# An attention and expert kernel: the first two units' start written out engine by engine, and the first unit's operands moved from SBUF straight to their partitions

## What is computed

```python
# x, ctx: (8, 256, 512); 16 heads of 16 channels
q = Wq @ layernorm(x) + bq;  k = Wk @ ctx + bk;  v = Wv @ ctx + bv
dot = q_head.T @ k_head / 4                      # 512 x 512 per head, masked
x = x + v_head @ (softmax(dot) * mask)
# then, for each of the 2048 rows (8 * 256) of x, with 8 experts:
h = layernorm(x); p = softmax(h @ gate.T); the two best experts, weights normalised
x = x + sum of weight * (silu(h @ w1g) * (h @ w1u)) @ w2
```

## Time and profile before

| | |
|---|---|
| median of 3 runs | 956.54 us (954.77 to 958.49) |
| the profiled execution, own time | 951.4 us |
| its span, first to last instruction | 949.6 us |
| PE busy (matmul) | 810.5 us, 85% |
| DVE busy | 538.6 us, 57% |
| POOL busy | 377.2 us, 40% |
| ACT busy | 316.7 us, 33% |
| mean granted TensorE clock | 0.949 |

### The profile page before, as it was taken

The page is one execution under the profiler, slowest core; times in us unless marked ns, Lnnn a source line. Parts: engine busy times, 40 slices in busy tenths (PEclk is TensorE's granted clock), DMA queues, the critical chain, the costliest instruction groups (busy, mean ns, idle before and its releaser), DMA issues. The chain is left out here.

```text
span 949.6 us, 12844 instructions
## 1 busy us (share of the span) xinstructions
PE 810.5 (85%) x3737; PEld 366.5 (39%) x3738; DVE 538.6 (57%) x1038; ACT 316.7 (33%) x615; POOL 377.2 (40%) x396
## 2 busy tenths in 40 slices
PE   2178999999998999999999983189999999999994
PEld 1022233333332333333333321155555555555552
DVE  2177888888887888887878722412323232322322
ACT  0003656555656555555556672000000000000000
POOL 5634445555755665566554324301111111111111
PEclk9677999999999999999999996589999999999998
DMA  4553467665866676657455322413635365363332
GB/s 120 169 177 113 145 206 222 187 221 177 268 195 193 210 224 197 201 181 210 134 177 156 125 92 90 143 46 67 147 58 155 57 156 146 66 146 62 59 66 34
DMA packets 84287, 137.69 MB, mean 145 GB/s; under 512 B 14600, under 2 KB 40520, under 8 KB 84240
## 3 DMA queue, kind: packets, MB, share of 16 engines
q1 hardware_dynamic: 68512, 107.97, 37.4%
q0 software_dynamic: 7744, 17.86, 9.6%
q10 hardware_dynamic: 7984, 11.28, 4.2%
HBM read 77.34 MB, written 59.36 MB: 144 GB/s over the span
## 5 line engine op out<-in xcount | busy, mean ns | idle before, releaser
L731 DVE TENSOR_REDUCE mx<-tile 128x2 f32<-128x1024 f32 x256 | 308.7, 1217 | 64.8 <-PE tile L985 61.3
L629 ACT ACTIVATE pr<-sc 128x512 f32<-128x512 f32 x512 | 268.8, 601 | 191.5 <-PE sc L972 189.0
L985 PE MATMUL tile<-qk 97*128 97x512 bf16 x512 | 157.2, 390 | 47.6 <-DVE mx L731 22.4
L1283 POOL DMA_INDIRECT out_dram<-y,ids x36 | 56.1, 1559 | 282.5 <-DVE ids L1208 278.4
L972 PE MATMUL sc<-qk 100*128 100x512 bf16 x512 | 154.6, 382 | 7.7 <-DMA qk<-mxt 5.1
L1001 PE MATMUL pvb<-pr,vp 128*32 128x512 f32 x1024 | 137.2, 608 | 0.0
L1263 ACT ACTIVATE sg<-gp 128x352 f32<-128x352 f32 x36 | 16.7, 465 | 291.3 <-PE up L1312 291.3
L1333 PE MATMUL dp<-wring,at 128*128 (+1 forms) x216 | 102.2, 609 | 13.4 <-DVE at L1218 13.4
L985 PEld LDWEIGHTS tile<-qk 97*128 97x128 bf16 x512 | 36.4, 98 | 185.7 <-DVE mx L731 83.0
L1312 PE MATMUL gp<-wring,xtile 128*128 x288 | 93.7, 469 | 2.1 <-DVE meta L1199 2.1
L554 POOL TENSOR_SCALAR parts<-qkf 128x512 bf16<-128x512 f32 x32 | 48.4, 1513 | 113.3 <-DVE qkf L812 112.4
(11 more groups left out here) (118 smaller groups left out, 723.9 us busy)
## 6 DMA issues: line engine op xcount, KB each, us to landing
qk<-stack_d SPq DMA_DIRECT2D x32, 768.0 KB
stack_d<-parts SPq DMA_DIRECT2D x32, 384.0 KB, 2.6
wring<-w_dram SPq DMA_DIRECT2D x32, 352.0 KB, 6.3
xl<-routed_d ACTq DMA_DIRECT2D x38, 257.0 KB, 2.7
stack_d<-parts SPq DMA_DIRECT2D x32, 256.0 KB, 2.9
pv_d<-ov SPq DMA_DIRECT2D x32, 256.0 KB, 4.1
xin<-x_dram SPq DMA_DIRECT2D x16, 256.0 KB, 5.7
cin<-ctxt_dram SPq DMA_DIRECT2D x8, 512.0 KB, 6.2
```

The costliest lines, as they stand in the source:

```text
L629: nc.scalar.activation(pr[s % 2][:, j, :], sc[(32 * u + 4 * s + j) % NSC][:, :], ACT.Exp, scale=SCALE).then_inc(exped.sem, 1)
L731: dve.tensor_reduce(mx[:, half(w), 2 * j:2 * j + 2], t[:, :, :], X, ALU.max, negate=True).then_inc(drained.sem, 1)
L985: last = nc.tensor.matmul(t[:, i, :], qs[half(w)][0:RAW_ROWS, h, c * P:c * P + P], ks[half(w)][0:RAW_ROWS, h, :], start=True, stop=True)
L1283: pool.indirect_dma_start(out, bass.IndirectOffsetOnAxis(ap=ids[:, k, :], axis=0), y[:, k, :], None, compute_op=ALU.add).then_inc(y_added, 16)
```

## The change

`tile_events` gives the tiles of units -2 and -1 in a new order: q and k of unit 1 (called "the second unit") come ahead of every raw score, the values of unit 0 after all its raw scores and the transposed maxima. Each engine's instructions up to unit -1 are written out, in an order of its own. The first unit's parts no longer pass through `stack_d`: SP (q) and ACT (k) start twelve transfers, one for each pair and side, from `parts` into 16 partitions of `qk[0]`, each as soon as its part exists. The first unit's k is split by DVE (`key_parts`), no longer by POOL. The constants that the start needs come first and have semaphores of their own. The five stores of `pad` are moved behind unit 1. SP's `keep_split(-1, 0)` is moved behind the transfer of the maxima. The diff, without its unchanged lines and the new semaphores' names:

```diff
@@ -102,6 +102,11 @@
+    if n == -2:
+        return ["q", "k"] + [("max", m) for m in range(LEAD)]
+    if n == -1:
+        return ([("max", m) for m in range(LEAD, NPAIR)]
+                + ["maxT", "v", ("max", 0), ("max", 1), "q", ("max", 2), ("max", 3), "k"])
@@ -278,8 +288,12 @@
-        split_kept = [Count(sem(f"split_kept{side}"), of(3 - side, "k"), 3 * 16) for side in range(2)]
-        stacked = [Count(sem(f"stacked{g}"), of(2 - g, "g"), 32) for g in range(2)]
+        split_kept = [Count(sem(f"split_kept{side}"), lambda n, w=3 - side: ["k"] if 0 < n + w < UNITS else [], 3 * 16)
+                      for side in range(2)]
+        stacked = [Count(sem(f"stacked{g}"), lambda n, w=2 - g: ["g"] if 0 < n + w < UNITS else [], 32)
+                   for g in range(2)]
+        first_moved = [sem(f"first_moved{side}") for side in range(2)]
+        first_mask = sem("first_mask")
@@ -302,13 +316,13 @@
+        early = ((io[:, :], iotas, io_in),
+                 (wq_s[:, :, :], wq.rearrange("(c p) o -> p c o", p=P), wq_in),
+                 (bqk[:, 0, :], bq, wq_in),
+                 (wk_s[:, :, :], wk.rearrange("(c p) o -> p c o", p=P), wk_in),
+                 (bqk[:, 1, :], bk, wk_in),
+                 (mall[:, :], mask, mask_in))
@@ -316,7 +330,16 @@
-        MADE = 8
+        MADE = 6
+        def first_stack(eng, u, side):
+            for part in range(3):
+                eng.wait_ge(split[side].sem, split[side].at(u, (0, 2, 3)[part]))
+                for i, pair in enumerate(PAIRS):
+                    if pair[side] == part:
+                        eng.dma_start(qk[0][i * D:i * D + D, side, :, :].rearrange("d h t -> d (h t)"),
+                                      parts[:, side, part, :]).then_inc(first_moved[side], 16)
@@ -415,7 +438,7 @@
-                if has(u + 1):
+                if has(u) and has(u + 1):
@@ -442,7 +465,7 @@
-                if has(u + 3):
+                if u >= 0 and has(u + 3):
@@ -454,22 +477,35 @@
-            for u in range(FIRST, -2):
-                unit(u)
-            sp.wait_ge(const_made, MADE)
-            sp.wait_ge(ones_made, 4)
+                if u == -1:
+                    keep_split(u, 0)
+            def pads():
+                for i in range(4):
+                    sp.dma_start(routed_d[E * CAP + i * P:E * CAP + (i + 1) * P, :], pad[:, :]
+                                 ).then_inc(padded, 16)
+                sp.dma_start(out[TOKENS:TOKENS + P, :], pad[:, 0:T]).then_inc(padded, 16)
+            load_x(-5)
+            load_x(-4)
+            load_ctx(-3)
+            sp.wait_ge(mask_made, 2)
+            load_x(-3)
+            load_x(-2)
-            for i in range(4):
-                sp.dma_start(routed_d[E * CAP + i * P:E * CAP + (i + 1) * P, :], pad[:, :]
-                             ).then_inc(padded, 16)
-            sp.dma_start(out[TOKENS:TOKENS + P, :], pad[:, 0:T]).then_inc(padded, 16)
-            for u in range(-2, LAST + 1):
+            sp.wait_ge(ones_made, 1)
+            for g in range(2):
+                sp.dma_start(qk[0][BIAS_ROW:BIAS_ROW + 1, :, 4 * g:4 * g + 4, :], mrow_d[0:1]).then_inc(first_mask, 16)
+            first_stack(sp, -3, 0)
+            keep_split(-2, 0)
+            for u in range(-1, LAST + 1):
+                if u == 1:
+                    sp.wait_ge(const_made, MADE)
+                    pads()
@@ -482,15 +518,15 @@
-            for h in range(2):
+            def ones_of(h):
-            pool.wait_ge(const_loaded, CONST)
+                pool.wait_ge(const_loaded, CONST)
@@ -549,6 +585,8 @@
+                if w == 1:
+                    pool.wait_ge(first_moved[side], 6 * 16)
@@ -576,7 +614,17 @@
-            for u in range(FIRST, LAST + 1):
+            ones_of(0)
+            pool.wait_ge(io_in, 16)
+            batch_rstd(-5)
+            batch_rstd(-4)
+            pool.wait_ge(normed.sem, normed.at(-4, "n"))
+            ones_of(1)
+            part(-3, 0)
+            batch_rstd(-3)
+            batch_rstd(-2)
+            part(-2, 0)
+            for u in range(-1, LAST + 1):
@@ -637,8 +685,12 @@
+            for dst, src, loaded in early:
+                act.dma_start(dst, src).then_inc(loaded, 16)
+            act.wait_ge(ones_made, 1)
+            first_stack(act, -2, 1)
@@ -924,20 +976,69 @@
-            unit(FIRST)
+            def key_parts(u):
+                w = u + 2
+                src = qkf[:, half(w), 1, :]
+                dve.wait_ge(drained.sem, drained.at(u - 1, "k"))
+                dve.tensor_reduce(parts[:, 1, 0, :], src.rearrange("p (t o) -> p t o", o=1), X, ALU.max
+                                  ).then_inc(split[1].sem, 1)
+                dve.wait_ge(split[1].sem, split[1].at(u, 0))
+                dve.tensor_tensor(rest[:, 1, :], src, parts[:, 1, 0, :], ALU.subtract).then_inc(split[1].sem, 1)
+                dve.wait_ge(split[1].sem, split[1].at(u, 1))
+                dve.tensor_reduce(parts[:, 1, 1, :], rest[:, 1, :].rearrange("p (t o) -> p t o", o=1), X, ALU.max
+                                  ).then_inc(split[1].sem, 1)
+                dve.wait_ge(split[1].sem, split[1].at(u, 2))
+                dve.tensor_tensor(parts[:, 1, 2, :], rest[:, 1, :], parts[:, 1, 1, :], ALU.subtract
+                                  ).then_inc(split[1].sem, 1)
-            dve.wait_ge(const_loaded, CONST)
+            for u in (-5, -4):
+                batch_stats(u, 0)
+                batch_stats(u, 1)
+            normalize(-5)
+            normalize(-4)
+            dve.wait_ge(mask_in, 16)
+            dve.tensor_copy(mrow[:, 0, :], mall[:, :]).then_inc(mask_made, 1)
+            dve.tensor_scalar(mrow[:, 1, :], mall[:, :], 1.0, NEG / SCALE, ALU.subtract, ALU.mult
+                              ).then_inc(mask_made, 1)
+            dve.wait_ge(io_in, 16)
+            dve.wait_ge(wq_in, 32)
+            projection_out(-3, 0)
+            dve.wait_ge(wk_in, 32)
+            projection_out(-3, 1)
+            key_parts(-2)
+            dve.wait_ge(const_loaded, CONST)
-            dve.tensor_copy(mrow[:, 0, :], mall[:, :]).then_inc(const_made, 1)
-            dve.tensor_scalar(mrow[:, 1, :], mall[:, :], 1.0, NEG / SCALE, ALU.subtract, ALU.mult
-                              ).then_inc(const_made, 1)
-            for u in range(FIRST + 1, LAST + 1):
+            projection_out(-2, 0)
+            projection_out(-2, 1)
+            for u in (-3, -2):
+                batch_stats(u, 0)
+                batch_stats(u, 1)
+            normalize(-3)
+            for j in range(LEAD):
+                maximum(-2, j)
+            normalize(-2)
+            for j in range(LEAD, NPAIR):
+                maximum(-1, j)
+            split_maxima(-1)
+            values_out(-1)
+            maximum(-1, 0)
+            maximum(-1, 1)
+            projection_out(-1, 0)
+            maximum(-1, 2)
+            batch_stats(-1, 0)
+            maximum(-1, 3)
+            batch_stats(-1, 1)
+            normalize(-1)
+            projection_out(-1, 1)
+            for u in range(LAST + 1):
@@ -946,9 +1047,6 @@
-            pe.wait_ge(const_made, MADE)
-            pe.wait_ge(ones_made, 4)
@@ -977,7 +1075,11 @@
-                if m % 8 == 0:
+                if m == 0 and w == 0:
+                    pe.wait_ge(first_mask, 32)
+                    pe.wait_ge(first_moved[0], 6 * 16)
+                    pe.wait_ge(first_moved[1], 6 * 16)
+                if m % 8 == 0 and w:
@@ -1103,7 +1205,27 @@
-            for u in range(FIRST, LAST + 1):
+            pe.wait_ge(wq_in, 32)
+            project(-3, 0)
+            pe.wait_ge(wk_in, 32)
+            project(-3, 1)
+            project(-2, 0)
+            project(-2, 1)
+            for m in range(LEAD):
+                raw_scores(-2, m)
+            for m in range(LEAD, NPAIR):
+                raw_scores(-1, m)
+            pe.wait_ge(const_made, MADE)
+            pe.wait_ge(ones_made, 4)
+            transpose_maxima(-1)
+            values(-1)
+            raw_scores(-1, 0)
+            raw_scores(-1, 1)
+            project(-1, 0)
+            raw_scores(-1, 2)
+            raw_scores(-1, 3)
+            project(-1, 1)
+            for u in range(LAST + 1):
```

More of the change, by code:

```diff
@@ L253, in attention @@
         pvb = st.enter_context(nc.psum_tensor("pvb", [P, T], F32))
+        io_in = sem("io_in")
+        mask_in = sem("mask_in")
+        wq_in = sem("wq_in")
+        wk_in = sem("wk_in")
         const_loaded = sem("const_loaded")
         const_made = sem("const_made")
+        mask_made = sem("mask_made")
         mrow_kept = sem("mrow_kept")
@@ L304, in attention @@
         block = st.enter_context(nc.Block())
-        const = ((idf[:, :], ident),
[L306 to L311, removed]
+        early = ((io[:, :], iotas, io_in),
[4 more added lines that the diff above has]
+                 (mall[:, :], mask, mask_in))
+        const = ((idf[:, :], ident),
                  (wv_s[:, :, :], wv.rearrange("(c p) o -> p c o", p=P)),
```

## The result

The changed kernel takes 947.94 us in the median of six runs (946.11 to 950.63), the kernel before 954.16 (952.79 to 958.49): ratio 0.9927, 95% interval 0.9902 to 0.9953. It is faster by 6.2 us where 25.8 were forecast, and 947.94 lies outside the range of 925 to 941.

A forecast was written before the change was run, and what follows sets the result against it. PE bounds units and experts, so the change is worth what it moves the first score: 25.4 + 7.9 - 5.0 - 2.5 = 25.8 us earlier, 956.5 to 930.7, call it 931; range 925 to 941.

The forecast's parts named there:

- Step 2: First raw score to transposed maxima: 20.6 us after the change against 28.5 before, a gain of 7.9.
- Step 3: Transposed maxima to first score: 12.0 us for 7.0, because values and third unit's q come here; a loss of 5.0.
- Step 4: Second unit's stack, needed for its first raw pair at 45.2, would land at 44.8: hidden by 0.4 us.
- Step 1: Start to first raw score: 22.1 against 47.47, a gain of 25.4 us, with 2.8 for the last transfer's landing.
- Rival B: Transfers landing on sixteen partitions are a narrow door, delaying the first unit's operands: 941 us, chance 0.08.
- Step 5: Unit 0: third unit's q split late, stack(1, 1) behind it, so PE stands before raw pair 8; 2.5 us taken.
- Step 6: Pad stores behind unit 1, ahead of stack(3, 1), which has 7 us spare: cost 0, at most 2 us.
- A: Rival: the second unit's chain decides, its stack 4 us late and unit 0's 4 more: 939 us, chance 0.17.
- D: Rival, slower: unit 0's debt is not paid off and PE stands before raw pair 8 in every unit: 968, chance 0.05.
- C: Rival, no gain: the twelve transfers are served one by one, start unchanged: 956 us, chance 0.04.

The follow-up runs named there:

- the run with ACT's order: The changed kernel, but ACT starts the first unit's six k transfers in pair order 5, 0, 3, 4, 1, 2, not 0, 3, 5, 1, 4, 2: 944.93 us.
- the run without it: The changed kernel, but SP issues stack(1, 1) ahead of keep_split(-1, 0), no longer behind it: 936.98 us, ratio 0.9805.
- The runs with the pads late: Five pad stores issued one to a unit in units 9 to 13: alone on the changed kernel 945.51 us; with stack(1, 1) ahead of keep_split(-1, 0) 936.35.
- the run through DRAM: The changed kernel, but the first unit's parts go through DRAM again, after all parts are made, all on SP: 947.02 us, ratio 0.9885.

## Why the prediction was wrong

**What held.** The mechanism and most terms. PE's start: 8.37 for 7.5 (it waited for a 1 KB bias, not for the weights). POOL's and DVE's parts: 18.8 and 19.3 for 17.9 and 18.7; a reduction over one element takes 0.69, a subtraction 0.69 alone and 1.10 and 1.37 beside POOL, so the overlap cost 0.4 and 0.7 for the 0.4 taken. (A second overlap stood in the kernel before, which the forecast didn't count: at 22.31 a normalisation took 0.54 beside POOL, whose split took 1.74 for 1.50.) The second subtraction ended at 19.31, 0.55 after POOL's own subtraction had ended at 18.76; in three other traces it is 16.25 after 15.71, with 1.29 to 1.66 for the one that waited. That agrees with the lock rule of the Trainium skill (SBUF — State Buffer, Who interferes with whom). The first ended at 17.18, while POOL's split ran from 16.03 to 17.53, which the rule doesn't give. Step 2, first raw to transposed maxima: 20.8 for 20.6. Step 3: 11.7 for 12.0. Step 4: the second unit's stack was issued at 46.65 and PE's first pair with it, at 56.66, did not wait.

**Step 1, the landing.** The term "issue 0.6, landing 2.8" was mis-sized. The transfers took 3.6 to 12.4 us to land, and the first raw score came at 32.3 for 22.1, that is 10.2 of the lost gain: 9.1 between the last issue and the raw score (11.9 for 2.8), the rest in parts and issue that were 1.1 later. The 2.8 came from transfers whose side in SBUF was all 128 partitions; these land on sixteen neighbours. Rival B (0.08) named this. It had two cases at a quarter of 251 GB/s for each quarter of the partitions: the quarters at the same time, 25 and 934, or all twelve transfers in turn, 41.5 and 950, and it took 941, which is a first raw score near 32.4. The measured 32.31 is that value, by luck of the middle: the transfers do share one rate, whichever quarter they go to, but it is 110 GB/s and not 63. The argument that nothing before lands on so few partitions was not quite so: the maxima and the mask rows do, in transfers of 8 KB that show no rate. Spreading the rows gives 8.2 back; the rate is then 229 to 265 GB/s and the time 940.67.

The Trainium skill (SBUF — State Buffer, Door 1: The DMA port swizzle) has 109 GB/s for partitions 0 to 15, and 104 measured; the 104 to 122 of the changed kernel's two traces are near it, at times above it. By its mapping sixteen partitions that are six apart reach 13 or 14 of the 16 ports, an estimated 354 GB/s or more; the 222 to 265 measured agree in kind and not in size. I had used the rule for each transfer's last 1.2 us and not for the queue of twelve. The Trainium skill (SBUF — State Buffer, Can I just issue two DMAs to hit both halves?) also says that two transfers to different halves serialize; the run with ACT's order agrees, 113 GB/s where the changed kernel has 109 to 122. The 150 to 155 GB/s measured with 32 neighbours lie below the 189 that the Trainium skill (SBUF — State Buffer, Door 1: The DMA port swizzle) gives for 32 in transfers of 1 MiB; why is open. What makes neighbours slow is thus shown by position, and the ports as its cause rest on that section of the Trainium skill alone.

**Step 5, the debt in unit 0.** Sized 2.5, measured 8.6 (lead 18.2 to 9.5). The sum for SP was right in kind: `stack(1, 1)` issued 8.2 after the first score (7.7 forecast), landed 14.6 after it (13.4). The need was wrong. I read pair 8 off the pair at 94.42. Counted in the kernel before from 83.83, pair 4, that one is pair 10; pair 8 starts at 91.58, 8.6 after the first score, not 11.4 (pairs 4 to 9):

```profile
83.83 1.06 PE L985 MATMUL tile<-qk 97*128 97x512 bf16 x2
...
85.87 0.60 PE L985 MATMUL tile<-qk 97*128 97x512 bf16 x2
...
86.85 0.60 PE L985 MATMUL tile<-qk 97*128 97x512 bf16 x2
...
88.92 0.60 PE L985 MATMUL tile<-qk 97*128 97x512 bf16 x2
...
91.58 0.59 PE L985 MATMUL tile<-qk 97*128 97x512 bf16 x2
...
93.54 0.60 PE L985 MATMUL tile<-qk 97*128 97x512 bf16 x2
```

With it the same sum gives a stop of 4.8 (13.4 - 8.6), and landing 1.2 later makes it the 6.1, near enough. The other 2.5 I put down to the clock, which stood at half after the stop and at full in the run without it. The forecast had no term for that.

**Step 6, the pads.** Cost 0, at most 2: 1 to 4 in the traces. The same misread row: the 7 us to spare were 4, against 2.5 of issue and 4 to 5 of data. The runs with the pads late moved unit 2 and not the timed median, so the size is a reading of traces.

**The sum.** 15.2 + 7.8 - 4.8 - 8.6 = 9.6 at unit 0's maxima; less the pads' 1 to 4 it is 5.6 to 8.6, and the medians differ by 6.2. Beside the kernel before on another occasion the changed kernel was 12.4 below it (945.89 and 958.27), so a difference of two medians has a few us of its own. Of the 19.6 us between the forecast gain and the measured one, the landing is 10.2, the debt in unit 0 is 6.1 (8.6 for 2.5), and the rest is about the pads' share. All failed towards too much gain. Two of the prediction's own signs of being wrong came: landings over 3.5 us and a stop in unit 2 behind the pads. A was right that a unit's stack would be late, but it was the third unit's debt in unit 0 and not the second unit's chain.

**D and C** did not come. The first raw score is 15.2 earlier, where C had it unchanged, and unit 1 takes 29.0 us for 29.4 before, so the debt was paid off within unit 0, where D had it in every unit. Single units of 33 to 35 us, in place of 31.8, occur in every trace, the kernel before's too (unit 7, 33.6), at changing places. What makes them was not tried.

## What to carry to other kernels

A transfer's duration may be taken from a row only if the row's transfer lies over the partitions in the same way; where a layout's row order is free, as in the sum of a matmul, give one transfer rows that are not neighbours (six apart here). When a start is pulled forward, count the instructions in the consumer's order up to the one that needs each transfer, and issue what is needed next before waiting for what is needed later. A stop of PE costs more than its length if the clock falls with it: 8.6 us for 6.1, 4.3 for 2.1, but 1.8 for 1.6, where it did not fall.

## What the runs showed of the hardware

- Transfers from SBUF to SBUF in packets of 1 KB, twelve on two queues: 101 to 128 GB/s into 16 neighbouring partitions each, 150 to 155 into 32, 222 to 265 into 16 that are six apart, 283 at the most into 96. The DMA engines count as busy in each (share 0.94 to 1.19; 1.16 at 111 GB/s, 0.94 at 283), so the busy share doesn't tell a high rate from two fifths of it.
- Two queues with different neighbourhoods at a time are no faster together (113 GB/s for 109 to 122).
- The same parts from 128 partitions to DRAM: 338 to 346 GB/s (20 to 24 us of the run through DRAM).
- After a stop of 6.1 us PE had half clock for 5.5 us and lost 2.5 more. After stops of 2.1 and 2.4 us the clock fell too, after stops of 0.9 to 1.6 us it did not. From the first raw scores to the values the clock is at 0.50 (32 to 57 us of the changed kernel), but there DVE's maxima set the pace: two take 2.3 us, four raw matmuls 1.87.
